# A Mamba and mixture-of-experts kernel on one core: no matmuls in the gap, first expert rows asked for in the dense block, another order in the opening, silu behind the eighth decay

## What is computed

```
# 1. an adapter per sequence, chosen by the sequence's language id
h = relu(x @ W1[id] + b1[id]);  y = x + h @ W2[id] + b2[id]
y = layernorm(y) * gamma[id] + beta[id]
# 2. four Mamba layers on y
for l in range(4):
    n = layernorm(y) * ln_w[l] + ln_b[l]
    xs, z = split(n @ W_in[l].T)
    u = silu(causal_conv4(xs) + conv_b[l])
    dt, B, C = split(u @ W_x[l].T);  dt = softplus(dt @ W_dt[l].T + b_dt[l])
    h_t = exp(dt_t * A) * h_(t-1) + dt_t * B_t * u_t        # 256 channels x 16 states, over 128 tokens
    y = y + ((sum_s h * C + u * Dp[l]) * silu(z)) @ W_out[l].T
x = x + y
# 3. a dense mixture: 8 gated experts and a shared one, all on every token
m = (1 - sg) * sum_e p[e] * (silu(x @ Wg[e]) * (x @ Wu[e])) @ Wd[e] + sg * shared(x)
# 4. a sparse mixture: every token goes to its top 2 of 8 experts, 1024 slots each
x = x + top2_moe(m, wg, gelu(. @ w_gate[e]) @ w_down[e])
```

## Time and profile before

| | us |
|---|---|
| median of three runs | 2602.84 |
| the profiled execution's own time | 2602.57 |
| its span in the trace | 2600.8 |
| PE busy | 2339.2 (90%) |
| DVE busy | 2047.0 (79%) |
| POOL busy | 2050.7 (79%) |
| ACT busy | 1609.3 (62%) |

### The profile page before, as it was taken

How to read it: one execution, slowest core, us unless ns; L and a number is a source line. 1 busy time by engine, 2 the same in 40 slices (tenths; PEclk the granted TensorE clock), 3 DMA queues, 4 the chain that set the end, 5 groups by cost and what they waited for, 6 DMA issues and landing times. The chain is left out here.

```text
span 2600.8 us, 22792 instructions
## 1 busy us (share of the span) xinstructions
PE 2339.2 (90%) x6094; PEld 1030.8 (40%) x6094; DVE 2047.0 (79%) x2011; ACT 1609.3 (62%) x2605; POOL 2050.7 (79%) x1264
## 2 busy tenths in 40 slices
PE   6688888888898889999999999999997999999994
PEld 4233333333333333333333333333333444444473
DVE  5799999999999999999999999999999243333121
ACT  3576777776777677777777777777775232232131
POOL 4599999999998899999999999999998233221266
PEclk9799999999999999999999999999999999999897
DMA  7455545564445766676667666766675400000533
GB/s 224 186 209 207 190 161 180 208 211 167 143 156 184 255 248 235 236 242 231 242 236 244 238 234 235 246 237 232 234 238 195 136 18 17 29 9 9 154 58 36
DMA packets 216931, 464.97 MB, mean 179 GB/s; under 512 B 29468, under 2 KB 109154, under 8 KB 216802
## 3 DMA queue, kind: packets, MB, share of 16 engines
q1 hardware_dynamic: 204818, 455.30, 51.6%
q0 software_dynamic: 11264, 7.98, 2.0%
q10 hardware_dynamic: 720, 0.23, 0.1%
HBM read 440.00 MB, written 23.99 MB: 178 GB/s over the span
## 5 line engine op out<-in xcount | busy, mean ns | idle before, releaser
L936 DVE TENSOR_TENSOR_SCAN hh<-decays,psdB 128x1024 f32<-128x1024 f32 x512 | 1165.9, 2283 | 62.0 <-ACT decays L736 20.3
L1075 POOL TENSOR_TENSOR products<-hh,Clo 128x1024 f32<-128x1024 f32 x408 | 962.6, 2363 | 94.1 <-DVE hh L936 93.2
L467 PE MATMUL psY<-products,ident 128*128 128x512 f32 x1674 | 824.8, 612 | 104.6 <-POOL products L1075 65.4
L736 ACT ACTIVATE decays<-dt,Acur 128x508 f32<-128x508 f32 x1024 | 667.7, 708 | 6.9 <-DVE hh L936 6.5
L467 PEld LDWEIGHTS psY<-products,ident 128*128 128x128 f32 x1674 | 306.8, 192 | 552.0 <-issue 358.4
L925 DVE TENSOR_TENSOR psdB<-psT,Blo 128x1024 f32<-128x1024 f32 x395 | 484.1, 1226 | 33.1 <-ACT psT L704 7.6
L1505 DVE TENSOR_TENSOR ac<-sg,d_bank 128x512 f32<-128x512 f32 x135 | 92.7, 688 | 222.9 <-PE d_bank L1352 204.2
L447 PE MATMUL psW<-xnT,wcur 128*128 128x512 f32 x496 | 227.5, 601 | 41.6 <-DMA diag<-diags_l 22.7
L1075 POOL TENSOR_TENSOR products<-hh,late 128x1024 f32<-128x1024 f32 x104 | 244.1, 2369 | 19.4 <-PE psY L467 19.4
L1079 POOL TENSOR_TENSOR products<-products 128x512 f32<-128x512 f32 x187 | 237.2, 1269 | 14.7
L1403 ACT ACTIVATE sg<-d_bank 128x512 f32<-128x512 f32 x135 | 80.6, 597 | 243.2 <-PE d_bank L1348 243.1
(11 more groups left out here) (219 smaller groups left out, 3061.8 us busy)
## 6 DMA issues: line engine op xcount, KB each, us to landing
Blo<-rows SPq DMA_DIRECT2D x280, 512.0 KB, 5.9
Clo<-rows SPq DMA_DIRECT2D x280, 512.0 KB, 5.1
late<-rows SPq DMA_DIRECT2D x104, 512.0 KB, 6.1
wcur<-taps_l SPq DMA_DIRECT2D x31, 512.0 KB
fw<-in_Wg SPq DMA_DIRECT2D x36, 256.0 KB, 5.3
fw<-in_Wu SPq DMA_DIRECT2D x36, 256.0 KB, 4.7
fw<-in_Wd SPq DMA_DIRECT2D x36, 256.0 KB, 5.5
disp<-fw SPq DMA_DIRECT2D x16, 528.0 KB, 7.3
```

What stands on the lines that cost most here:

```text
L467: ins = pe.matmul(psY[:, :], lhsT=ident[:, :], rhs=gg[k % NGB][:, j, :], start=False, stop=(k % NK == NK - 1 and j == last - 1))
L736: ins = act.activation(dA[k % NDA][:, j, :, 1:T], dt[i % 2][:, c, :, 1:T], ACT.Exp, scale=Acur[i % 2][:, s:s + 1])
L936: dve.tensor_tensor_scan(out=hh[k % NHB][:, :, :].rearrange("p c t -> p (c t)"), data0=dA[k % NDA][:, :, :, :].rearrange("p c q t -> p (c ...
L1075: ins = pool.tensor_tensor(gg[k % NGB][:, :, :], hh[k % NHB][:, :, :], tile(Clo, Chi, slot(i, s)), ALU.mult)
```

## The change

Four edits. (1) In the dense block PE's 32 matmuls and the wait ahead of them are gone. (2) The wait for the scattered rows and the two loads of expert 0's first rows move from the start of the sparse block to the end of SP's queue in the dense block; the buffers `dx` and the semaphore `x_first` are allocated for both blocks. (3) In iterations below 15 ACT's silu stands at step 8 instead of 7, ahead of the decays of step 8 and behind those of step 7, and the bcdt copy at step 9 instead of 8. (4) In the opening x of group 0 has its own load and semaphore ahead of the ids' wait; group 2's loads go ahead of the first weights and group 4's ahead of the other layers'; PE runs 12 matmuls on the identity before the first turn; PE, ACT and POOL take the groups and the preparation of iteration 0 in another order.

```diff
+ACT_EARLY = {**ACT_AT, 7: ["z1"], 8: ["silu"], 9: ["bcdt"]}
...
 def load_adapter(g):
     at_least(sp, h_ok, g + 1 - NAB)
-    sp.dma_start(xg[p], A["x"][G * g:G * (g + 1)]...).then_inc(ad_ld[p], 16)
+    if g > 0:
+        sp.dma_start(xg[p], A["x"][G * g:G * (g + 1)]...).then_inc(ad_ld[p], 16)
...
 sp.dma_start(ids[:, :], A["ids"]).then_inc(ids_ld, 16)
+sp.dma_start(xg[0], A["x"][0:G]...).then_inc(x0_ld, 16)
 sp.wait_ge(ids_ld, 16)
 load_adapter(0)
 load_adapter(1)
+load_adapter(2)
 first_weights()
-load_adapter(2)
 load_adapter(3)
+load_adapter(4)
 other_layers()
-load_adapter(4)
 save_first()
...
 # PE: turn_x(0) waits for x0_ld, hidden(0) for the adapter rows
 pe.wait_ge(cst, 1)
+for r in range(12):
+    pe.matmul(psW[:, 0:128], lhsT=ident[:, :], rhs=ident[:, :], start=True, stop=True)
 turn_x(0)
 hidden(0)
 condition(0)
 turn_x(1)
 hidden(1)
+condition(1)
 turn_x(2)
-condition(1)
 hidden(2)
 transposes(0)
 condition(2)
 turn_x(3)
+hidden(3)
 pre(0, "x0")
+condition(3)
+turn_x(4)
+hidden(4)
 pre(0, "x1")
-hidden(3)
-turn_x(4)
-condition(3)
-hidden(4)
-pre(0, "z0")
-pre(0, "z1")
 condition(4)
 turn_x(5)
+hidden(5)
+pre(0, "z0")
+condition(5)
+pre(0, "z1")
+turn_x(6)
 pre(0, "bcdt")
-hidden(5)
-turn_x(6)
-condition(5)
 hidden(6)
 pre(0, "dt0")
+condition(6)
 turn_x(7)
-condition(6)
+hidden(7)
 pre(0, "dt1")
-hidden(7)
 condition(7)
...
 # ACT: copy_xT(3), relu(3), first_u(0), copy_xT(4), relu(4), first_u(1), centre(1),
 #      copy_xT(5), relu(5), first_z(0), first_z(1), copy_xT(6), first_rows, relu(6),
 #      first_step(0), copy_xT(7), relu(7), first_step(1)
 # POOL: adapter_rstd(4), taps(1), adapter_rstd(5), taps(2), adapter_rstd(6), taps(3)
...
-for what in ACT_AT.get(k, ()):
+for what in (ACT_EARLY if i < FIRST else ACT_AT).get(k, ()):
...
 # dense block, SP's last instructions
+for p in range(2):
+    sp.wait_ge(K["scat"][p], 16 * 2 * NSEQ // 2)
+for c in range(2):
+    sp.dma_start(K["dx"][c][0][:, 0:HC, :], A["disp"][c, 0, 0:CAP // NHT]...).then_inc(K["x_first"], 16)
...
 # dense block, PE's last instructions
-pe.wait_ge(silued, CR + NST * NDT)
-for r in range(32):
-    pe.matmul(psG[r % 2][:, :], lhsT=ident[:, :], rhs=wgu[:, 0, 0, :], start=True, stop=True)
```

More of the change, by code:

```diff
@@ L22 @@
 NCH = CAP // 128
+NHT = CAP // 512
+HC = NCH // NHT
 EPS = 1e-5
@@ L211, in wave_phase @@
             sem("a_" + n) for n in "xT_up xT_ok hid_up hid_ok cond_up cond_ok stats_ok var_ok rs h_ok neg".split())
-        a_st, pch, half_ln, half_dt, half_dtu = (sem(n) for n in "a_st pch half_ln half_dt half_dtu".split())
+        a_st, pch, half_ln, half_dt, half_dtu, x0_ld = (sem(n) for n in "a_st pch half_ln half_dt half_dtu x0_ld".split())
         ad_ld = [sem(f"ad_ld{p}") for p in range(NAB)]
@@ L245, in at_least, with rows_of @@
                 eng.wait_ge(sm, v)
+        def rows_of(g):
+            return 16 * (1 + G) * (g // NAB + 1) - (16 if g % NAB == 0 else 0)
         def residents(d):
@@ L355, in _ @@
                 sp.dma_start(ids[:, :], A["ids"]).then_inc(ids_ld, 16)
+                sp.dma_start(xg[0], A["x"][0:G].rearrange("b t d -> t b d")).then_inc(x0_ld, 16)
                 sp.wait_ge(ids_ld, 16)
@@ L404, in turn_x @@
                     p = g % NAB
-                    pe.wait_ge(ad_ld[p], 16 * (1 + G) * (g // NAB + 1))
+                    if g == 0:
+                        pe.wait_ge(x0_ld, 16)
+                    else:
+                        pe.wait_ge(ad_ld[p], rows_of(g))
                     at_least(pe, xT_ok, g - 1)
@@ L413, in hidden @@
                     pe.wait_ge(xT_ok, g + 1)
+                    if g == 0:
+                        pe.wait_ge(ad_ld[p], rows_of(0))
                     at_least(pe, hid_ok, g)
@@ L793, in _ @@
                 copy_xT(3)
+                relu(3)
                 first_u(0)
-                centre(1)
+                copy_xT(4)
+                relu(4)
                 first_u(1)
@@ L798, in _ @@
                 act.sem_inc(silu_ok, 1)
-                relu(3)
-                copy_xT(4)
-                relu(4)
+                centre(1)
+                copy_xT(5)
+                relu(5)
                 first_z(0)
                 first_z(1)
-                copy_xT(5)
+                copy_xT(6)
                 first_rows()
-                relu(5)
-                copy_xT(6)
                 relu(6)
@@ L810, in _ @@
                 copy_xT(7)
+                relu(7)
                 first_step(1)
-                relu(7)
                 act.preload_act_table_set(LNEXP)
@@ L1098, in _ @@
                 adapter_rstd(3)
+                adapter_rstd(4)
                 taps(1)
-                adapter_rstd(4)
+                adapter_rstd(5)
                 taps(2)
-                adapter_rstd(5)
+                adapter_rstd(6)
                 taps(3)
-                adapter_rstd(6)
                 adapter_rstd(7)
@@ L1525, in sem @@
             return ctx.enter_context(nc.semaphore("e_" + name))
-        NHT = CAP // 512
-        HC = NCH // NHT
         wg, wd, w_ld = K["ewg"], K["ewd"], K["ew_ld"]
@@ L1531, in sparse_phase @@
         BATCH = [0, 1, 2, 2, 3, 3, 3, 3]
-        dx = [[sb(f"dx{c}_{p}", [128, NCH, RW]) for p in range(NE)] for c in range(2)]
+        dx = K["dx"]
         dT = [sb(f"dT{b}", [128, 512]) for b in range(2)]
@@ L1538, in sparse_phase @@
         psT, psH, psE = bank[0:2], bank[2:6], bank[6:8]
-        x_ld, x_first = [sem(f"x_ld{b}") for b in range(4)], sem("x_first")
+        x_ld, x_first = [sem(f"x_ld{b}") for b in range(4)], K["x_first"]
         picked, homed, trans, copied, upped, gelud, downed, evac, added = (
@@ L1557, in _ @@
             def _(sp):
-                for p in range(2):
-                    sp.wait_ge(K["scat"][p], 16 * 2 * NSEQ // 2)
                 def load_rows(e):
                     lo = HC if e == 0 else 0
-                    if e == 0:
-                        for c in range(2):
-                            sp.dma_start(dx[c][e][:, 0:HC, :], A["disp"][c, e, 0:CAP // NHT].rearrange("(n p) d -> p n d", p=128)).then_inc(x_first, 16)
                     for c in range(2):
@@ L1722, in mega @@
             "ew_ld": [ctx.enter_context(nc.semaphore(f"ew_ld{p}")) for p in range(2)],
+            "x_first": ctx.enter_context(nc.semaphore("x_first")),
             "wbc": sb(ctx, "wbc", [128, NE1, NSEQ]),
@@ L1740, in mega @@
             K["ewd"] = [sb(c5, f"ewd{p}", [128, NF, D]) for p in range(2)]
+            K["dx"] = [[sb(c5, f"dx{c}_{e}", [128, NCH, RW]) for e in range(NE)] for c in range(2)]
             K["first"] = sb(c5, "first", [128, NE, NCH], i32)
```

3 lines of the change are left out of this document (2 added, 1 removed).

## The result

The changed kernel takes 2574.14 us (median of 4 runs, 2571.89 to 2577.76) where the one before takes 2602.07 in the same session (4 runs, 2599.39 to 2603.69): 27.9 us less between the medians. The ratio of the runs is 0.9896, with a 95% interval from 0.988 to 0.9912, or 23 to 31 us. The forecast was 2567 within 2557 to 2577. The profiled execution of after is the longest of its four: 2577.76, with a span of 2575.9, 24.9 less than the span before.

The account below looks back on a forecast made before the run. Bounds were taken by stretch: DMA in the opening, DVE and POOL side by side in the iterations, PE in the dense block. Gap -17.1, silu -18.2 and opening 0 took 2602.57 to 2567 us, range 2562 to 2572, wide 2557 to 2577.

Parts of the forecast that it names:

- The gap: Between dense and sparse block: DVE's first selection of rows starts 17.1 us earlier, from -19.4 to -13.
- the engines meet at about 2421.9: At the dense block's end: all engines are through 2.5 us before the first rows arrive, so the rows set the start.
- The clock at the start of the sparse block: PE's first work there runs at half clock as before, worth 0; bounds 2.3 us gained, 4 us lost.
- The silu: In the iterations' loop: step 7's stall goes, step 9's margin of 0.3 us is narrowest; -18.2 us in sum.
- in iterations 0 and 1 the silu stands later against DVE by 1.06 us: First two iterations: stalls of 2.45 us shrink to 0.6, a gain of 1.8 each, 3.6 together.
- Row store 56.5 against 56.35: the opening is worth 0: In the opening: SP's row store, which sets the DMA chain's end, stays in place, so no gain or loss.
- bcdt at about 54.1: In the opening: PE's bcdt product starts at about 54.1 in place of 51.8, its copy done at 56.5.
- nearest is the row at 23.01: In the opening: TensorE had not left half clock by 23.01 us and the new order keeps that, so 0.
- the bound of +3: In the opening: 3 us lost if everything runs at half clock until x0 and short stages wait more.
- the stall only moves: Rival in the iterations' loop: only half the silu's gain comes, 2576 us; chance 0.12.
- The opening gains: Rival in the opening: 12 early matmuls and earlier loads bring 6 us, 2561 us; chance 0.14.
- slower than before: Rival in the iterations: late softplus holds POOL and DVE, 2 us in each of 15, 2615 us; chance 0.02.

Follow-up runs that it names:

- mm_only: The kernel before without the 32 matmuls in the gap, first rows still requested in the sparse block; first selection 10.37 us behind the last scatter's issue, no time given.
- gap_only: The kernel before with only the gap's edits: no matmuls there, first rows requested in the dense block; 14.8 us faster.
- open_only: The kernel before with only the opening's edit; 2.5 us slower, with a ratio interval that touches 1.
- gap_refill: gap_silu with 16 of the 32 matmuls put back in the gap; first up product 6.46 us, no kernel time given.
- silu_only: The kernel before with only the silu moved behind the eighth step's decays in iterations below 15, as first stated; 13.7 us faster.
- gap_silu: The changed kernel with the opening of before, so only the gap's and the silu's edits; same time as the whole change within the measurement.
- whole_again: The changed kernel itself, unaltered, run and profiled again on another chip; 2573.48 us.
- all_order_only: The changed kernel with only the new group order left of the opening's edit: no 12 matmuls, no separate x, old loads; time like gap_silu's.

## Why the prediction was right or wrong

**The gap: right, 16.4 us for 17.1.** The request stands 2.37 us behind the last scatter, where the sum had 2.4. The step that failed is "the engines meet at about 2421.9", T + 3.6, put 2.5 us before the rows: they meet at T + 6.5, behind the rows, and now this meeting releases the selection. That the price was near is luck: 6.83 us from scatter to selection instead of 6.1, because the meeting came only 0.4 us behind the rows' landing. What follows from it is different: asking for the rows still earlier would bring nothing here.

**The clock at the start of the sparse block: right.** Half clock in both, and the up product some 0.2 us shorter than before (6.0 to 6.4 us for 6.6 in all kernels without matmuls there), far inside the bounds of 2.3 us gained and 4 lost. What the sum left out is the rest of the sparse block, 1 us longer in most of these kernels.

**The silu: right in kind, 2 to 4.6 us short in size.** No stall of step 7, no wait at step 9, margins of 1.0 and 0.6 where 0.87 and 0.3 were expected, POOL now full (52.80 of 53.22 us). The iteration is 53.22 instead of the forecast 53.1: POOL and DVE give 1.30, not 1.39. Iterations 0 and 1 gave 2.8 and 2.4 against before (53.8 and, undisturbed, 53.2 us from 56.6 and 55.6). With 11 x 1.30 that makes 19.5. Two terms of the sum were off, and both hang on TensorE's clock, which falls to half in the midst of the iterations, now for less than 4 us, now for about 7.

The first is the step "in iterations 0 and 1 the silu stands later against DVE by 1.06 us". For iteration 1 this isn't the schedule: before and mm_only have two of the long stretches in iteration 0 (122 to 129 and 139 to 146 us in before), gap_only and open_only have none, and only the first two have the second stall of 2.45 and the wait at 156.50.

The second is that the sum has no term for such stretches behind the change. In after, the clock by window, then what ACT and the DVE do behind it:

```profile
302.00:309.00 7.00, 6.22 (x9) 2.10 (x8) 6.82 (x5) 4.86 (x8) 7.00 (x5) 0.51 0.83 300
```

```profile
315.50 0.60 ACT L726 ACTIVATE yg<-psY 128x512 f32<-128x512 f32 x1 [6.41 <-PE psY L481]
317.79 1.02 ACT L740 ACTIVATE psdB<-fw 128x1024 f32<-128x1024 f32 x1
...
319.01 2.29 DVE L952 TENSOR_TENSOR_SCAN hh<-decays,psdB 128x1024 f32<-128x1024 f32 x1 [0.98 <-ACT psdB L740]
```

PE's sums come late, ACT's copy of them has waited 6.41 us instead of the 4.22 of an undisturbed iteration, the given term is moved late, and the scan waits for it. Such an iteration is 54.3 and the next 53.8 us instead of 53.2: 1.7 us together. The nine profiles with the new silu have two long stretches each in iterations 0 to 12, and behind every one of the 18 the DVE waits, 0.55 to 1.16 us for the given term, or, in after and gap_refill where it falls into iteration 12, 1.88 and 1.85 us for psT in iteration 13. Behind the short stretches there is no such wait. So 19.5 - 3.4 = 16.1 in silu_only, gap_silu and whole_again, which measure 16.15, 16.2 and 16.3, and 19.5 - 1.7 - 0.35 - 1.88 = 15.6 in after (15.7 measured; the 0.35 is a small loss in iteration 7). Whether the idleness of before was a cushion against these stretches is not shown: no profile with the old silu has a long one in iterations 1 to 12, and the two of iteration 0 go with a loss of 2.5 us together. Why the new place of the silu goes with more of them is open.

**The opening: wrong.** The step "Row store 56.5 against 56.35: the opening is worth 0" put three things in one number. Measured at the row store, each from single profiles: the loads -2.2 us, the order +3.4 with the old loads and +4.4 with the new ones (57.08 in whole_again against 52.65), the 12 matmuls either about -1.4 (all_noorder 52.65 against 54.09) or, at half clock, +4. The whole is 57.08 in one profile and 60.89 in the other. "bcdt at about 54.1" was right where the clock held (54.52 in whole_again). Calling the clock undecided was right; what was wrong is "nearest is the row at 23.01", the choice of one state where this kernel has both, and the bound of +3, which 60.89 passes by 1.5.

**The start of the dense block: not in the sum.** Between the statistics of i=15 and the later table load, before takes 1120.5 us and after 1123.3; nothing in it was edited. The first dense products on PE, before and then after:

```profile
2037.74 1.10 PE L1348 MATMUL d_bank<-h_res,fw 128*128 128x512 f32 x2 [2.03 <-ACTq L1377]
2038.67 1.02 PE L1352 MATMUL d_bank<-xw,fw 128*128 128x512 f32 x2
```

```profile
2027.84 1.10 PE L1368 MATMUL d_bank<-h_res,fw 128*128 128x512 f32 x2 [2.00 <-ACTq L1394]
2028.77 1.53 PE L1372 MATMUL d_bank<-xw,fw 128*128 128x512 f32 x2
2030.09 1.92 PE L1368 MATMUL d_bank<-h_res,fw 128*128 128x512 f32 x2
```

A pair of products takes 1.92 us instead of 1.02: the clock is at half again (0.57 in 2029 to 2033), and this is the 1.53 of the table. The 1.29 ahead of the first table load are of the same kind. There four pairs of PE's products at the end of the iterations (L511 and L521 before) take 1.67, 1.02, 1.13 and 1.02 us before (from 2022.27) and 1.91, 1.91, 1.50 and 1.02 after (from 2011.13), because a stretch at half clock ends later against the work. The thirteen profiles fall in two kinds: in seven this stretch takes 1120.2 to 1120.7 us, in six 1123.2 to 1123.7. Every kernel of the second kind has edits 1 to 3, but all_order_only has them too and is of the first, and so are silu_only and gap_refill with edit 3. So the 2.9 us often go with the changed kernel, and not always; what decides where the clock falls is open.

**The sum.** Forecast -35.3, measured -27.9 in the medians. By whole_again, whose -28.5 is a usual run, the 6.8 us short are 0.7 in the gap, 1.9 in the silu, nothing in the opening, 3.2 at the dense start and 1.1 in the sparse block; in the profile of after the opening's 4.5 come on top. So the measured 2574 lies outside the forecast's own range (2562 to 2572) and inside the wide one, which had been widened for other mishaps ("the stall only moves" gave 2576); no rival names the clock in the iterations and at the dense start, and that the result is in the range is in part luck. "The opening gains" and "slower than before" did not come true. The opening does gain without the new order: all_noorder starts iteration 0's statistics 3.4 us earlier than before.

## What to carry to other kernels

When the engine that sets the end of a stage has finished, look at when the engines meet at the block's border before pricing an earlier request: here the border, not the data, came last. A stall read from one profile can be the clock's doing and not the schedule's: look whether a second profile of the same loop has it before counting it as a gain, and in a loop without slack leave a term for the waits that the clock's falls bring. Moving short stages in front of the one product that a DMA chain waits for delays the chain (here bcdt by 5.4 us), whatever it does for the stages behind.

The version that the runs point to is all_noorder, the whole change without the new order in the opening: 2569.77 us (4 runs, 2567.87 to 2570.55), below every run of after. The intervals of the two ratios overlap (0.9861 to 0.9892 and 0.988 to 0.9912), so the advantage is likely and not proven. Without its 12 matmuls it is the same within the measurement (2570.98), and no profile without them had the half clock ahead of bcdt that three of five had with them.

## What the runs showed of the hardware

- Behind GpSimd's indirect DMAs the engines meet at the end of a block 5.6 us after the issue of the last one has ended (T + 6.5, in mm_only without anything of SP's pending), and 0.3 us after PE where PE was last (before: 2437.5 to 2437.84).
- 16 matmuls with 2.14 us of idleness behind them do not keep TensorE at 2.4 GHz through the next product (6.46 us in gap_refill).
- TensorE's granted clock falls to half in the midst of busy iterations (0.51 in 302 to 309 of after, with PE busy for 5.03 of the 7 us ahead at 1.00). Stretches of about 7 us were each followed by a wait in the loop with the new silu, 18 of 18 in nine profiles, and cost about 1.7 us; those under 4 us cost nothing that shows.
- In profiles without the 12 matmuls the granted clock reads 1.00 from the start, though four transposes take 1.1 us at 10.3 and 0.66 at 43.8; with them it reads 0.50 in 20 to 30 for the same 1.1. In the opening the duration of a known instruction tells the clock, not the column.
- One program, profiled twice, had its first iteration's scan of step 4 start 4.6 us apart (104.48 and 99.90), and the medians of a kernel hide which of the two a run had.
